# Value products one per step in two of every three steps, and a ring of 24 exponentials, in a fused attention kernel

## The reference

```
query = heads(ct_q @ Wu_q + b) + heads(rope(ct_q @ Wq_r + b))      # ct_q = x @ Wd_q + b
key   = heads(ct_kv @ Wu_k + b) + heads(rope(x @ Wk_r + b))        # ct_kv = x @ Wd_kv + b
value = heads(ct_kv @ Wu_v + b)
attn  = softmax(query @ key.T / sqrt(16 + 128 + 128))
x = layernorm(x + (attn @ value) @ Wo + b)
x = layernorm(x + int8_linear(x))      # x rounded to int8 with one scale for all of it
```

## Time and profile before

| | |
|---|---|
| median of three runs | 1998.19 us |
| the profiled execution | 1997.78 us |
| its span, first to last instruction | 1995.9 us |
| mean granted clock of TensorE | 0.981 of full |
| busy: TensorE (PE), ScalarE (ACT), VectorE (DVE) | 1806.7, 1827.3, 1578.7 us |
| ScalarE's exponentials | 1860, from 157.3 us to 1899.7 us |

### The profile page before, as it was taken

The page is one execution under the profiler, slowest core; times in us unless marked ns, Lnnn a source line. Parts: engine busy times, 40 slices in busy tenths (PEclk is TensorE's granted clock), DMA queues, the critical chain, the costliest instruction groups (busy, mean ns, idle before and its releaser), DMA issues.

```text
span 1995.9 us, 31796 instructions
## 1 busy us (share of the span) xinstructions
PE 1806.7 (91%) x13009; PEld 490.0 (25%) x13009; DVE 1578.7 (79%) x1500; ACT 1827.3 (92%) x2026; POOL 167.3 (8%) x134
## 2 busy tenths in 40 slices
PE   8967999999999999999999999999999999999965
PEld 3431222222222222222222222222222222222234
DVE  3654887988887888888788888788988988888548
ACT  4448999999999999999999999999999999999925
POOL 5723500000000000000000000000000300000012
PEclk9998999999999999999999999999999999999977
DMA  4654111110111111111121000111111100110012
GB/s 163 215 170 163 25 25 25 25 25 18 21 22 19 21 25 25 24 25 25 25 67 25 19 18 17 22 25 25 25 25 25 25 21 21 21 21 17 1 44 85
DMA packets 165484, 81.48 MB, mean 41 GB/s; under 512 B 130205, under 2 KB 146717, under 8 KB 164857
## 3 DMA queue, kind: packets, MB, share of 16 engines
q1 hardware_dynamic: 164024, 78.11, 15.0%
q10 hardware_dynamic: 1312, 1.32, 0.2%
HBM read 48.83 MB, written 29.23 MB: 39 GB/s over the span
## 4 chain that ended last, share of the span: by engine, by line
ACT 66%; PE 13%; issue 10%; DVE 4%; POOL 2%; DMA 2%; SPq 1%; ACTq 0%; DVEq 0%; POOLq 0%
ACT arena L797 53%; ACT parts_or_sums L797 13%; PE PS L598 7%; PE PS L555 4%; PE PS L637 2%; PE PS L1041 1%; POOL arena L1360 1%; DVE arena L857 1%; DVE bn L725 1%; DMA arena<-arena 1%; DMA Qst<-parts_or_sums 1%; POOL arena L1359 1%; POOL arena L1362 1%; DVE arena L1651 1%; DMA arena<-head_out 0%
## 5 line engine op out<-in xcount | busy, mean ns | idle before, releaser
L797 ACT ACTIVATE arena<-PS 128x1024 f32<-128x1024 f32 x1488 | 1395.0, 1038 | 30.5 <-PE PS L555 29.1
L598 PE MATMUL PS<-arena,Vh 128*32 128x512 f32 x6704 | 1001.2, 600 | 0.8 <-DVE arena L857 0.4
L555 PE MATMUL PS<-Qst,Kst 49*128 49x512 f16 x4096 | 691.3, 384 | 126.8 <-ACT arena L797 77.1
L857 DVE SCALAR_TENSOR_TENSOR arena<-arena 128x2048 f32<-128x2048 f32 x282 | 646.5, 2292 | 0.1
L833 DVE TENSOR_SCALAR arena<-PS 128x512 int32<-128x512 f32 x376 | 259.3, 690 | 286.1 <-PE PS L555 278.1
L555 PEld LDWEIGHTS PS<-Qst,Kst 49*128 49x128 f16 x4096 | 178.5, 93 | 945.5 <-ACT arena L797 710.8
L598 PE MATMUL PS<-parts_or_sums,Vh 128*32 128x512 f32 x1488 | 366.1, 600 | 0.0
L797 ACT ACTIVATE parts_or_sums<-PS 128x1024 f32<-128x1024 f32 x372 | 360.9, 1037 | 3.8 <-PE PS L555 3.4
L598 PEld LDWEIGHTS PS<-arena,Vh 128*32 128x32 f32 x6704 | 195.0, 109 | 340.5 <-issue 331.1
L853 DVE SCALAR_TENSOR_TENSOR arena<-arena 128x2048 f32<-128x2048 f32 x94 | 216.0, 2298 | 0.0
L841 DVE TENSOR_SCALAR arena<-arena 128x2048 int32<-128x2048 int32 x94 | 115.7, 1231 | 7.3
(11 more groups left out here) (115 smaller groups left out, 615.4 us busy)
## 6 DMA issues: line engine op xcount, KB each, us to landing
Kst<-k_halves SPq DMA_DIRECT2D x64, 128.0 KB
Qst<-q_halves SPq DMA_DIRECT2D x64, 128.0 KB
Vh<-head_values SPq DMA_DIRECT2D x30, 256.0 KB, 4.4
arena<-xT_dram SPq DMA_DIRECT2D x8, 512.0 KB, 5.1
k_halves<-parts_or_sums SPq DMA_DIRECT2D x16, 256.0 KB, 2.4
k_whole<-arena SPq DMA_DIRECT2D x8, 512.0 KB, 3.3
q_halves<-parts_or_sums SPq DMA_DIRECT2D x16, 256.0 KB, 3.2
q_whole<-arena SPq DMA_DIRECT2D x8, 512.0 KB, 4.4
```

What stands on the lines that cost most here:

```text
L555: return nc.tensor.matmul(out, Kst[par][low:low + HK + 1, at:at + 128], Qst[par][low:low + HK + 1, j * CH:(j + 1) * CH], start=True, stop= ...
L598: last = nc.tensor.matmul(bank(value_bank(t))[32 * j:32 * j + 32, :], Vh[t % 2][:, kt, :], moving, start=kt == first, stop=kt == last_kt)
L797: nc.scalar.activation(ring(at, k), bank(g % SLOTS * SLOT, k), ACT.Exp, scale=EXP_SCALE).then_inc(a.exp, 1)
L857: last = nc.vector.scalar_tensor_tensor(out=t, in0=t, scalar=POLY[3 - j], in1=power if j == 3 else mantissa, op0=ALU.add, op1=ALU.mult)
```

## The change

The value products go to steps that are 0 or 1 mod 3, at most one to a step, in place of one or two in each step that is 0 mod 3. VectorE's blocks go to steps that are 2 or 1 mod 3, as before (two expressions in place of one). `LAG` falls from 6 to 4, `BEFORE` and `BEHIND` by one each, `URGENT` from 6 to 4, and the ring has 24 blocks, all of them in `arena`.

```diff
-RING = 30
+RING = 24
...
-LAG = 6
-VALUE_PHASE = 0
+LAG = 4
+VALUE_PHASES = (0, 1)
+BLOCK_PHASES = (2, 1)
 FIRST_BLOCKS = 14
-BEFORE = 4
-BEHIND = 5
+BEFORE = 3
+BEHIND = 4
 VECTOR_LATE = 4
-URGENT = 6
+URGENT = 4
...
     for k in range(KT):
         s = HEAD_STEP[t] + LAG + k * length // KT
-        s += (VALUE_PHASE - s) % SLOTS
+        s = max(s, steps[-1] + 1 if steps else 0)
+        while s % SLOTS not in VALUE_PHASES:
+            s += 1
         steps.append(min(s, STEPS_ALL))
...
             s = first + (last - first) * k // (n - 1)
-            s += s % SLOTS == VALUE_PHASE and k < n - 1
+            s += s % SLOTS not in BLOCK_PHASES and k < n - 1
             steps.append(s)
```

## The result

The changed kernel takes 1988.11 us (median of five runs, 1986.62 to 1989.43) against 1998.19; the ratio to before is 0.9951, with a 95% interval of 0.9936 to 0.9965. So it gains 0.5%, some 10 us, where 23 were forecast. The profiled execution took 1989.43 us, its span is 1987.6 us (1995.9 before).

A forecast was written before the change was run, and what follows sets the result against it. ScalarE was taken as the bound. From the profiled 1997.8 us, 22.3 for the attention and 0.9 for the end were subtracted, giving 1974.6; with 0.4 to the median, 1975, range 1958 to 1992.

The forecast's parts named there:

- VectorE: nothing: VectorE's bits and polynomials end 0.85 us sooner, paying for value products four steps behind; no change, 0 to 2 us.
- Bursts halved: Value products on TensorE, one at a time: ScalarE loses 12.4 ns a step against 24.4, gain 22.3 us.
- dense groups: Groups of three attention steps with a value product in both of the first two; 403 by the changed tables.
- Rival A: Attention: lateness isn't handed on as summed, so pairs of dense groups lose nothing; 1965, or 1952 without head-end loss; chance 0.17.
- head ends: Where attention heads end: three in 174 steps, each adding two score pairs of 0.21 us more each.
- Output projections: nothing: The 16 projections on TensorE, 1.15 us each: loss about 14.5 us in sum, 14 before.
- my walk: Lateness rule followed through 58 groups of three steps: loss of 2.16 us in 174 steps.
- The ring: Ring of 24 blocks for ScalarE's exponentials: nothing gained, up to 3 us of loss.
- The end: After the attention: VectorE's last block comes 0.85 us sooner within its step; gain 0.9 us.
- More switches: TensorE: 1022 bursts in place of 618 cost 99 us more of its time, hidden in part in 289 us of waiting.
- Rival B: Attention: lateness of dense groups isn't cleared; slower, about 2021 at most, 2012 at the low end; chance 0.05.
- The waits that were to show it: TensorE's waits for exponentials, from 300 to 1000 us: down by about a third, to some 200 us.

The follow-up runs named there:

- placing alone: Kernel before with only the changed placing of value products and blocks; LAG, BEFORE, BEHIND, URGENT and RING as before: 1987.89 us, ratio 0.9937.
- constants-only kernel: Kernel before with only the changed LAG, BEFORE, BEHIND, URGENT and RING, products placed as before: 2026.05 us, ratio 1.0146.

## Why the prediction was wrong

The sign was right, and the time lies in the range; the size was not, 23 us forecast against 10. The step that failed is *VectorE: nothing*: a term put at 0 that cost 7.5 us of the 13.9 missing in the attention; the others are 2.3 at the output projections, 2.2 in the plain steps and 1.9 in the first 120. By its steps:

- *Bursts halved:* right where attention runs alone. 0.9188 us a step against a forecast of 0.917; the other 1312 steps gave 13.6 of the 15.8 us. But the number was right for a reason that I had only half. I took 0.905 as ScalarE's pace and built the 12.4 ns above it from late starts of pairs of dense groups. ScalarE's own pace is 0.917 by its ends, the same under three loads on TensorE. So what I called a loss left over is mostly the floor. A hint of it stood in the earlier trace rows, durations from 1015 to 1117 ns for one and the same instruction. Rival A, 1965 with no loss at the pairs, was never to be had. The late starts themselves came where and as often as forecast: the changed kernel has 62 (over 0.03 us) in the 590 steps from 330 to 920, 61 of them at the third step of a group, and fifteen pairs and three head ends in 174 steps would be 61. And placing alone gave only 10.2 of the 13.6 us; part of the gain came from the shorter distances, which have no term in the sum.
- *VectorE: nothing:* this is the step that failed. The two stretches, where 1.4 us were to be gained, lost 6.1: 7.5 of the 14 us missing in the attention. I worked out its cover for blocks, polynomials and norms, which recur in each head, from one head's end. I didn't lay the side jobs (`hooks` in the code) beside the new distances: jobs of 3.4 and 2.3 us that don't recur. Products of VectorE's tiles four steps behind (30 in place of 11), and three steps from the last block to the next head's first product in place of four, left no room for either. TensorE waits, ScalarE waits, and the clock halves. Moving them gave 6.1 us back.
- *Output projections: nothing:* I had them lose 0.5 us more; that the gain of 12 ns a step doesn't reach their stretch I had not allowed for. It gave 0.9 us where 3.2 were in the sum. Against the pace around them the 16 cost 16.4 us (14.0 before); my walk had 14.5. Those beside a product in a dense group make ScalarE up to 1.22 us late at a single step, where I had 0.7 to 1.1.
- *The ring:* the changed kernel loses at most 2 us by it, inside the bound. The constants-only kernel shows that it would have cost 23.5 us with the old placing: a reason for the new one that I didn't see.
- *The end:* 1.7 us against 0.9, which proves nothing: this part varies between the kernels from 91.6 to 96.2 us, and between two profiles of the changed kernel from 94.5 to 92.8. The start of the attention varies from 156.5 to 160.8, with no edit there.
- *More switches:* start to start a burst costs what I had. In the lines above scores take 0.32 us to the product (392.16 to 392.48) and the product 1.00 to the next scores (393.48), together 1.32 where the forecast has 1.33. TensorE's busy time grew by 53 us, not 99; busy time isn't the sum of such distances, and where the rest lies wasn't pursued.
- *Rival B's upper end:* a slip in the sum. 187 pairs at 0.3 us are 56, and 1998 + 56 - 23 is 2031, not 2021. The range doesn't use it.

The waits that were to show it did not: from 408 to 1000 us TensorE's weight loads wait 351 us for exponentials, 0.59 of the time. In the earlier trace rows it is 289 us of 700, and a further 73 us for exponentials in `parts_or_sums` that I left out: 0.52. I had forecast a fall. That the exponentials' later ends make up the difference is argued, not shown.

The first 120 steps (off by 1.9 us) stay open; two profiles of the changed kernel differ there by 0.8 us.

## What to carry to other kernels

When a schedule is drawn tighter, lay every job that occurs only once or twice beside the new distances, not only those that recur: here jobs of 2.3 and 3.4 us took back 6 of the 14 us that the attention would have gained. Read an engine's pace from the ends as well as from the starts; where durations grow along a run of even starts, the starts are ahead of the work and the pace is the slower one. And multiply a gain only over the stretches in which its bound is the one at work.

## What the runs showed of the hardware

An ACTIVATE of 128 x 1024 starts 0.904 us behind the last when its scores are there, and lasts 13 ns longer each time, up to 1.28 us in the plain stretch; ends are 0.917 us apart.

TensorE's granted clock fell to 1.2 GHz behind waits of 2.58 and 1.89 us inside an attention otherwise at 2.4 GHz, and stayed there for 3.4 us each time; in the constants-only kernel it did so behind a wait of 2.42 us. Far more surprising, it stayed at 1.2 GHz nearly all through the attention when the value products were bf16 in place of fp32, with TensorE busy at that clock for 693 of 700 us from 300 to 1000 us:

```profile
300.00:1000.00 700.00, 692.78 (x3354) 134.42 (x3351) 592.99 (x501) 697.66 (x761) 0.00 (x0) 0.50 0.11 23
```

The value products were 4096 matmuls in place of 8192 there. From its start to the next scores a product took 0.55 us at 1.2 GHz (600.10 to 600.65 us), against 1.00 at 2.4 GHz in the changed kernel. Less work for TensorE went with a lower clock, and ScalarE still ran at its own pace. Why the clock wasn't granted is open.
